# Two-layer block on one core: another order of loads and first norms, feed-forward woven in from the fifth attention piece

## The reference

```python
x = x + attn0(norm(x)) + ffn0(norm(x))
x = x + attn1(norm(x)) + ffn1(norm(x))
# layer 0 attention: linear attention, 16 heads of 16
qp, kp = elu(x @ q_w.T + q_b) + 1, elu(x @ k_w.T + k_b) + 1
kv = einsum('bhsd,bhse->bhde', kp, v)
attn = einsum('bhsd,bhde->bhse', qp, kv) / (qp . kp.sum(s) + 1e-6)
out = attn @ o_w.T + o_b
# layer 0 feed-forward: weights cut to -1, 0, 1 times mean|W|
hidden = silu(x @ wu.T) * (x @ wg.T);  y = hidden @ wd.T
# layer 1 attention: rotary positions, softmax over 1024 keys, 16 heads of 16
# layer 1 feed-forward: sign vectors, Walsh-Hadamard transforms and scales
# around up, gate (1024 wide) and down, with silu(gate) * up
```

## Time and profile before

| | |
|---|---|
| median of runs | 751.56 us |
| profiled execution | 753.33 us |
| its span | 751.2 us |
| TensorE busy | 700.9 us (93%) |
| VectorE busy | 532.0 us (71%) |
| ScalarE, GpSimd busy | 438.4 us (58%), 293.8 us (39%) |
| mean granted TensorE clock | 0.977 |

### The profile page before, as it was taken

The page is one execution under the profiler, slowest core; times in us unless marked ns, Lnnn a source line. Parts: engine busy times, 40 slices in busy tenths (PEclk is TensorE's granted clock), DMA queues, the critical chain, the costliest instruction groups (busy, mean ns, idle before and its releaser), DMA issues.

```text
span 751.2 us, 10957 instructions
## 1 busy us (share of the span) xinstructions
PE 700.9 (93%) x4186; PEld 441.4 (59%) x4186; DVE 532.0 (71%) x872; ACT 438.4 (58%) x600; POOL 293.8 (39%) x269
## 2 busy tenths in 40 slices
PE   4779899969988989999999998999999999999998
PEld 3567798957667868777667674333333433333445
DVE  4886766565658646678878878888988288888315
ACT  2462334445544633342332435999998899999883
POOL 1145755445755945334343541122233214322410
PEclk9898999989999999999999999999999999999999
DMA  6155101003005462252201110344435244433231
GB/s 256 56 175 179 53 0 57 1 2 108 5 1 168 133 232 85 85 196 71 99 1 57 57 57 24 130 142 142 141 89 170 89 163 146 145 100 94 91 89 57
DMA packets 25847, 74.13 MB, mean 99 GB/s; under 512 B 4620, under 2 KB 5996, under 8 KB 24964
## 3 DMA queue, kind: packets, MB, share of 16 engines
q1 hardware_dynamic: 21268, 65.37, 26.0%
q0 software_dynamic: 3808, 7.60, 3.5%
q10 hardware_dynamic: 720, 0.48, 0.2%
HBM read 54.54 MB, written 23.06 MB: 103 GB/s over the span
## 4 chain that ended last, share of the span: by engine, by line
PE 60%; POOL 2%; DVE 2%; ACT 1%; issue 1%; DMA 1%; SPq 0%; DVEq 0%; POOLq 0%; ACTq 0%
PE PS L1022 17%; PE PS L760 12%; PE PS L1008 12%; PE PS L766 8%; PE PS L991 6%; PE PS L981 5%; DVE mx L1321 1%; POOL sg L1631 1%; ACT P L1530 1%; DMA scr_k<-spl 1%; POOL rot L1651 1%; POOL rot L1652 0%; PE PS L997 0%; ACT spl L1512 0%; ACT us L1495 0%
## 5 line engine op out<-in xcount | busy, mean ns | idle before, releaser
L1530 ACT ACTIVATE P<-PS 128x1024 f32<-128x1024 f32 x256 | 249.1, 1023 | 30.8 <-PE PS L1008 30.6
L1328 DVE TENSOR_REDUCE mx<-PS 128x1 f32<-128x512 f32 x300 | 189.2, 682 | 33.1 <-PE PS L991 31.5
L1321 DVE TENSOR_REDUCE mx<-PS 128x2 f32<-128x1024 f32 x106 | 124.8, 1221 | 37.4 <-PE PS L981 37.1
L1022 PE MATMUL PS<-P,VV 128*32 128x512 f32 x1024 | 137.3, 608 | 0.1
L1622 POOL TENSOR_TENSOR hl<-sg,hh 128x512 fp32r<-128x512 f32 x64 | 83.7, 1307 | 135.7 <-ACT hh L1492 68.3
L1008 PEld LDWEIGHTS PS<-QS,KS 64*128 64x128 f32 x512 | 48.6, 183 | 124.1 <-ACT P L1530 111.0
L1008 PE MATMUL PS<-QS,KS 64*128 64x512 f32 x512 | 117.0, 456 | 2.3 <-DVE mx L1321 1.8
L991 PE MATMUL PS<-KM,QM 64*128 64x512 f32 x300 | 81.7, 398 | 0.0
L1486 ACT ACTIVATE sg<-PS,cols 128x512 f32<-128x512 f32 x32 | 22.0, 688 | 81.0 <-PE PS L760 81.0
L1631 POOL TENSOR_TENSOR sg<-sg,us 128x512 f32<-128x512 f32 x32 | 42.1, 1314 | 37.5 <-ACT us L1495 37.5
L760 PE MATMUL PS<-XH,UGH 128*128 128x512 f32 x128 | 54.2, 423 | 1.6 <-ACT us L1495 0.8
(11 more groups left out here) (210 smaller groups left out, 1391.8 us busy)
## 6 DMA issues: line engine op xcount, KB each, us to landing
QM<-scr_q SPq DMA_DIRECT2D x16, 512.0 KB, 4.2
KM<-scr_k SPq DMA_DIRECT2D x16, 512.0 KB, 5.3
QS<-scr_q SPq DMA_DIRECT2D x16, 512.0 KB, 4.3
KS<-scr_k SPq DMA_DIRECT2D x16, 512.0 KB, 5.2
scr_q<-spl SPq DMA_DIRECT2D x24, 256.0 KB, 3.2
scr_k<-spl SPq DMA_DIRECT2D x24, 256.0 KB, 3.4
scr_o<-OE POOLq DMA_DIRECT2D x14, 256.0 KB, 3.0
stg<-in_tern SPq DMA_DIRECT2D x3, 1024.0 KB, 4.9
```

The costliest lines, as they stand in the source:

```text
L1022: i = e.matmul(PS[32 * c:32 * c + 32, 7, :], v_head(8 * b + kt, 2 * j + c // 2), P[s % 4][:, chunk(c // 2 + 2 * (c % 2))], start=(kt == 0) ...
L1321: e.tensor_reduce(mx[p % 2][:, :, qt, half], PS[:, b:b + 2, :], AX.X, ALU.max).then_inc(q["mx"], 2)
L1328: e.tensor_reduce(mx[p % 2][:, h, qt, half:half + 1], bank[b], AX.X, ALU.max).then_inc(q["mx"], 1)
L1530: e.activation(P[s % 4][:, half * 1024:(half + 1) * 1024], PS[:, b:b + 2, :].rearrange("p b n -> p (b n)"), ACT.Exp).then_inc(q["ex"], 1)
```

## The change

Seven edits:

1. Loads: tokens 0 and 1, then `wa0`, then tokens 2 and 3, then all three ternary weights at once, into four staging buffers instead of two. Waits ahead of the loads go.
2. First norms: both norms 0 and 1 stand on VectorE ahead of the first `XL`; the remainder `W0L` is made on GpSimd in two parts (the columns of keys and values first), not on VectorE; norms 2 and 3 come later, and their transposes go to banks 7 and 6, those of the down products.
3. Ternary cuts are spread differently, with `tern_scale` in the ring `pf`. The first gate comes after five side pieces and waits for the cut of `TU` alone; `up` waits for `TG`, `down` for `TD`.
4. `RATE0` is 1.0 instead of 0.8. The end of the key-value sums (`kv_end`) is spread over more pieces.
5. Layer 1's norms are scaled in two pieces of two tiles (`ln_norm`, `ln_norm_b`).
6. Query products of attention 0 are read by VectorE first and then by ScalarE, and `qk` waits for the first of the two `W1` remainders only.
7. TensorE gets products of ones that nothing reads: 20 instead of 8 at the start, and 4 and 2 ahead of the first two score steps (`busy`).

The core of the diff:

```diff
-FIRST = 12
-RATE0 = 0.8
+RATE0 = 1.0
...
@@ layernorm
         put("ln_norm", n)
         yield
+        if n >= 4:
+            put("ln_norm_b", n)
+            yield
         put("ln_turn", n, ring.next(), ring.next())
...
@@ kv_end
         put("kv_sum", 8 * b + 7)
+        yield
+        yield
         for tt in range(8 * b + 5, 8 * b + 8):
             put("kv_out", tt)
+        yield
         put("kv_sums", b)
+        yield
         yield
...
+    def beside(sides):
+        front = [(tn[2], 2), (ln0[2], 1), (tn[2], 1), (tn[2], 1), (ln0[2], 1), (tn[2], 1), (ln0[3], 1), (ln0[3], 1)]
+        for n, _ in enumerate(sides):
+            if n < len(front):
+                step(*front[n])
+            if n in (9, 16):
+                put("bias", 0, 2 + n // 16)
+            yield
...
-    ln0 = [layernorm(c, pf) for c in range(NCH)]
+    ln0 = [layernorm(c, pf if c < 2 else Ring([7, 6])) for c in range(NCH)]
...
-    weave(main(0), sd0, RATE0)
+    weave(main(0), beside(sd0), RATE0)
...
+        if s < 2:
+            put("busy", 4 - 2 * s, mxr.peek())
...
-        stg = [sb(f"stg{i}", 174 + 8 * i, [128, 2048]) for i in range(2)]
+        stg = [sb(f"stg{i}", (174, 182, 156, 147)[i], [128, 2048]) for i in range(4)]
...
@@ sync, start
+                tokens(0)
+                tokens(1)
                 e.dma_start(stg[0][:, :], wa0).then_inc(d["st0"], 16)
+                tokens(2)
+                tokens(3)
+                for n in range(3):
+                    i, _ = STAGE[f"tern{n}"]
+                    e.dma_start(stg[i][:, :], tern[n]).then_inc(d[f"st{i}"], 16)
...
@@ tensor
-                sums(bank[7][:, 0:128], [(ONES[:, :], ONES[:, :])] * 8)
+                sums(bank[7][:, 0:128], [(ONES[:, :], ONES[:, :])] * 20)
+            def busy(n, b, *after):
+                claim(b)
+                if after:
+                    e.wait_ge(q[after[0]], after[1])
+                sums(bank[b][:, 0:128], [(ONES[:, :], ONES[:, :])] * n)
...
@@ tensor, gate and up of layer 0; qk
-                        e.wait_ge(q["tt"], 4)
+                        e.wait_ge(q["tt"], 2)
...
+                    if m == 0 and c == 0:
+                        e.wait_ge(q["tt"], 4)
...
-                        e.wait_ge(q["w1l"], 2)
+                        e.wait_ge(q["w1l"], 1)
...
@@ scalar, ln_norm
-                for t in range(4):
+                for t in (2, 3) if second else (0, 1):
...
@@ gpsimd
+            def w0l(i):
+                raw = stg[0][:, :].rearrange("p (k n) -> p k n", k=2)
+                e.wait_ge(q["w0h"], 1)
+                for cs in ((slice(256, 768),), (slice(0, 256), slice(768, 1024)))[i]:
+                    e.tensor_tensor(W0L[:, :, cs], raw[:, :, cs], r32(W0H[:, :, cs]), ALU.subtract).then_inc(q["w0l"], 1)
```

## The result

The changed kernel takes 756.82 us (median of 5 runs, 753.65 to 757.1), the kernel before 750.76 beside it: ratio 1.0066, 95% interval 1.0047 to 1.0085. By the ratio it is 5 us slower (6.1 between the two medians); I had forecast 731 us, 20 us faster. Its profiled execution is its shortest, 753.65 us with a span of 751.6; the spans of the other four are 754.5 to 755.0. The profiled execution of the kernel before, 753.33 with a span of 751.2, is longer than all five of its timed runs. So the two profiles differ by 0.4 us only: they show why the forecast gain of 20 us did not come, and not the whole of the 5 us between the medians.

The account below looks back on a forecast made before the run. TensorE's work plus its idle and low-clock time bounds the kernel. Terms 5 + 4.5 + 6 + 1.4 + 4 + 1.5 + 2 - 4 = 20.4 us off 753.33 give 732.9, 1.8 lower by median: 731 us, range 726 to 738.

Parts of the forecast that it names:

- The start, gain 5: First 58 us, edits 1 to 4: earlier weights and first product at 14.5 gain 5 us, bounds -3 and 11.
- the first wait, 4.5: At 78.27: the 2.85 us wait for an attention division and its half clock go, gain 4.5 us.
- I take 12: masked sums at 64.3: Start's VectorE list from 15.2: 37.1 us of work plus 12 us of waiting puts the masked sums at 64.3.
- Norms in halves, gain 6: Layer 1's norms, stage 156 to 172: shorter chain and work before the turn gain 6 us, bounds 3.9 and 8.9.
- Single waits: Waits at 186.31, 210.71 and 226.49 go, gaining 1.4, 4 and 1.5 us.
- Now `qk` comes ahead of that turn: At 226.49: the queries' bank no longer waits for a norm's `XL`, gain 1.5 us, bounds 0 and 2.1.
- What comes new, 4: Side pieces 25% denser leave engines less slack: 4 us lost, range 0 to 8, one wait with tail.
- First scores, gain 2: Stage 456 to 466: earlier maxima and ones remove the `mx` wait and low clock, gain 2 us.
- The fourth rival: 25 to 60 us: early gates queue ahead of products VectorE needs; five 5.8 us waits give 760 us; chance 8%.
- The first: Rival: start stays bound by VectorE and the port, losing the 5; density costs 8, not 4: 740 us; chance 20%.
- The second: Rival: the stage at 264 grows by one 5 us wait with tail, giving 736 us; chance 10%.
- the third: Rival: the start does better, VectorE waiting only 6 us as before, giving 725 us; chance 12%.

Follow-up runs that it names:

- e15: Changed kernel with spread transforms and GpSimd's first low part waiting for VectorE's norm of chunk 1, plus ScalarE's second |W| sum one place earlier: 743.29 us, ratio 0.9889.
- e5: Changed kernel with chunk 3's first norm moved one side step earlier on VectorE, ahead of a cut of the down weights: 758.41 us, ratio 1.008.
- e16: e15 with GpSimd's bias for chunk 1 moved seventeen pieces later, behind the first cut of the down weights: 743.01 us, ratio 0.9891.
- e18: e16 with norm and turn of chunk 3 one piece earlier and the second cut of the down weights behind them: 746.74 us, ratio 0.9943.
- e8: Changed kernel with GpSimd's low part of the first weights waiting until VectorE has written the norm of chunk 1: 756.12 us, ratio 1.0048.
- e11: Changed kernel with query and key transforms spread, five feed-forward steps each instead of four: 746.72 us, ratio 0.9933.
- e10: Kernel before with norms in halves, waits on the first low part only, and ones before the first two score steps; old start kept: 747.14 us, ratio 0.9937.
- e13: e10 with the first weights' load issued behind the first two token chunks instead of all four: 742.56 us, ratio 0.9879.
- e4: Kernel before with layer 1's norms scaled in two pieces of two tiles, a main piece between: 750.61 us, ratio 0.9985.
- e17: e11 with the norm of chunk 2 two steps later, so turn 6 stays behind the second transform: 748.57 us, ratio 0.9954.
- e7: Changed kernel with eight products of ones at the start and none ahead of the score steps: 756.17 us, ratio 1.006.
- e1: Changed kernel with layer 1's norm of chunk 2 begun three steps sooner, putting turn 6 ahead of the second query and key transform: 753.89 us, ratio 1.0034.
- e9: Changed kernel with the three order changes of e1, e5 and e8 together: 753.94 us, ratio 1.0027.

## Why the prediction was wrong, step by step

The likeliest case, its first three rivals and the range all failed; the side with 8% came. The amounts below are from the table of stages, profiled execution against profiled execution; they close to about 2 us. Two steps failed most: the new order of `qk` and turn 6 with the denser transforms, and VectorE's list at the start, in which work was left out.

- **The start, gain 5, and the first wait, 4.5.** The landing (9.1 us), the high part, the first product and the vanished wait of the earlier trace rows came as forecast. Idle and clock together fell by 5.0, and 2.9 us more ones are counted as work, so 2.1 of 9.5. The step that failed is "37.1 us, so 52.3 if it never waits" with "I take 12: masked sums at 64.3". VectorE came to the masked sums at 69.36. Up to there it was busy 43.8 us and not 37.1, and waited 10.3 and not 12; so the work was mis-sized, not the waiting. The stretch in the columns of the earlier trace rows, then two of its groups on VectorE (count, busy us, mean ns):

```profile
15.20:69.36 54.16, 40.22 (x179) 32.76 (x179) 43.83 (x93) 24.63 (x43) 21.67 (x14) 0.84 0.35 134
```

```profile
L1207 DVE SCALAR_TENSOR_TENSOR TD<-stg,s,TD 128x1024 fp32r<-128x1024 f32 x2 | 3.6, 1796 | 0.0
L1199 DVE TENSOR_SCALAR TD<-stg,s 128x2048 fp32r<-128x2048 f32 x1 | 1.3, 1287 | 0.0
```

Of the 6.7 us that the sum lacks, 4.9 are the cuts of `TD`. They stood behind the masked sums before (66.19 to 73.98 us) and stand ahead of them now: I had used that as a gain at 78.27 and not charged it here. Another 1.4 is the scaling of norms 2 and 3, 4.7 us instead of 3.3. With 69.4 in the place of 64.3, the 6.4 us of gain become 1.3. Inside the list TensorE is stopped by single pieces: the sum of |TG| behind exponentials in ScalarE's order (e15: 2.6 us), chunk 3's norm and low part (7.1 us of idle, and 7.0 to 8.5 in the orders of e5, e16 and e18). In the runs the GpSimd collision of e8 adds 2.4 to 3.9 by the first gate. By medians the whole new start is worth 0.4 us (e11 against e10), where one of its edits, the load, is worth 4.6 on the old start (e13).

- **Norms in halves, gain 6, measured 1.1** (e4). "The chain is 1.0 us shorter" held to 0.03 us. The step that failed is "now lie between the norm and its turn": the same gate, attention product, up and down stood there in the list of the kernel before too, so they could hide nothing more, and in e4 the wait still ends on the attention's division. The tail of half clock stayed. In the changed kernel the wait of the earlier trace rows is gone, but three smaller ones stand around it, and the stage loses 0.6 more than before:

```profile
151.10 0.70 PE L878 MATMUL PS<-kvb,QP 128*128 128x136 f32 x4 [1.93 <-POOL QP L1638]
159.21 0.73 PE L878 MATMUL PS<-kvb,QP 128*128 128x136 f32 x4 [1.30 <-DVE XL L1176]
174.86 1.06 PE L825 MATMUL PS<-IDN,XD 128*128 128x128 f32 x8 [2.44 <-issue]
```

- **Single waits.** The one at 186 went, 1.4 us. The one for `w1l` is worth 2.3 alone (forecast 4): its tail went, and an equal one came at 225.4; with the norms in halves as well (e10) neither is there. "Now `qk` comes ahead of that turn", priced as a gain of 1.5, is the step that failed worst: it put turn 6 behind a transform's rotations, and TensorE waited 6.33 us there. The stage loses 12.9 instead of 7.2, 5.6 worse where 5.5 better was forecast.
- **What comes new, 4.** The cause is the one I named, "side pieces are 25% denser", and its price is 7 to 8 us in the transforms' stage alone (e11, e17). I priced density as one wait at a place unknown, though the list of pieces shows the place: from the first of the four transforms to the last it is 28 pieces instead of 38.
- **First scores, gain 2.** Idle and clock fell by 3.0, less 1.4 for the ones: 1.6. The size is right, and e7 tells by what: it has no ones there, and neither a wait for `mx` nor a low clock. So the maxima that end earlier suffice, as I had said, and the ones did nothing that shows.
- **The fourth rival** had the sign but not the mechanism: two idles over 3 us between 20 and 60, not four or five, and the loss that decides lies at 205 to 227. The span from the first score product to the end moved by 1.4 us (291.9 against 293.3), as allowed; the mean clock is 0.977, not 0.985. Neither sign that I had named for being wrong appeared: both looked elsewhere than at 205 to 227.
- **The other rivals.** The first comes nearest by mechanism: waits ate most of the start's gain and density cost 7 to 8. Its 740 failed because it kept the other terms, the norms' 6 and the single waits above all. The second, a longer stage at 264, did not come: from the first to the third chunk's down products it is 7.3 us before and after. Nor did the third.
- **GpSimd beside VectorE.** My prediction looked for stretched operations among `zk` sums and cuts. The norm's scaling `XC` is stretched too: its 16 operations took 405 to 414 ns in the kernel before, one took 2433 in e1, and the four at 39.00 took 3.34 us together, two of them 1385 each. The Trainium skill (SBUF — State Buffer, Who interferes with whom) counts `tensor_scalar` among the operations that can contend with GpSimd; the traces agree.
- **The clock.** The prediction said that the trace disagrees with the Trainium skill's figure for the ramp. The seven low stretches of the kernel before all lie behind waits, from 31 us on, and cost 14.9 us; they are no ramp at a kernel's start, so the trace doesn't contradict that figure.

## What to carry to other kernels

When a change makes a side stream denser or moves one piece past another, write down for each place where it now stands close who frees its banks and what that engine has queued ahead of it; a price for "some new wait" is no substitute. List what else has moved ahead of each point that you time: here 4.9 us of cuts were counted as gone from one place and not as come to another. Test a bundle of edits apart: here three of its parts together gave 4.7 us and a single load 4.6 more, while the whole lost 5. In these runs an idle that ended on a loaded engine's work moved when the order changed (e1, e5, e9, e18); look for the one that ends on an engine that was itself idle, as ScalarE was for 5.58 us.

## What the runs showed of the hardware

A VectorE operation of 0.17 us, on 128 by 4 numbers, took 2.05 us in e1 beside GpSimd's bias (timeline of e1):

```profile
20.59 2.38 POOL L1619 TENSOR_TENSOR X<-X,OB 128x1024 f32<-128x1024 f32 x1 [4.55 <-DMA OB<-in_ob]
...
20.94 2.05 DVE L1161 TENSOR_SCALAR rstd<-mv 128x4 f32<-128x4 f32 x1
```

And where the collision can fall either way it makes the same program take two times: TensorE's wait at 10.6 us was 1.78 in one execution and 3.65 in the next, so the median and the profiled execution need not show the same case. The changed kernel's other four runs were 3 us longer than its profiled one. The 2.4 to 3.9 us by which the collision puts off the first gate would cover that, but these runs were not traced, and e8, which removes the collision, kept a median of 756.12. So what makes them longer stays open.
